# First expert tile in other PSUM banks, and a later place for GpSimd's last product of a stage

## What is computed

```python
# state-space block, per batch: 512 channels, 16 states, 512 time steps
u     = silu(conv4(in_proj @ ctx))
delta = softplus(dt_proj @ dt_low + bias)
state = state * exp(delta * A) + (delta * u) * B      # a scan over time
y     = sum over the 16 states of state * C, plus D * u
x     = x + tanh(g) * (y * silu(layernorm(x)))
# layer 0's feed-forward: 16 experts, 4 for each token, and a shared one
x     = x + tanh(g) * (sum of w_e * ((silu(x @ G_e) * (x @ U_e)) @ D_e) + shared)
# layer 1's feed-forward: a dense matmul and low-rank experts, 2 of 8
```

## Time and profile before

| | |
|---|---|
| median of 3 runs | 1559.41 us (1557.27 to 1560.66) |
| profiled execution: time, span | 1560.78 us, 1559.0 us |
| TensorE busy | 1263.5 us (81%) |
| VectorE busy | 1413.8 us (91%) |
| ScalarE busy | 835.8 us (54%) |
| GpSimd busy | 794.4 us (51%) |
| mean granted TensorE clock | 0.922 of full |
| DMA | 264.27 MB, mean 170 GB/s |

### The profile page before, as it was taken

The page is one execution under the profiler, slowest core; times in us unless marked ns, Lnnn a source line. Parts: engine busy times, 40 slices in busy tenths (PEclk is TensorE's granted clock), DMA queues, the critical chain, the costliest instruction groups (busy, mean ns, idle before and its releaser), DMA issues.

```text
span 1559.0 us, 13944 instructions
## 1 busy us (share of the span) xinstructions
PE 1263.5 (81%) x4244; PEld 701.1 (45%) x4244; DVE 1413.8 (91%) x1462; ACT 835.8 (54%) x1341; POOL 794.4 (51%) x413
## 2 busy tenths in 40 slices
PE   6785687799699868987869999889998889923888
PEld 2322232343244324442526666566665666612444
DVE  4999999999999999988896999999899999977894
ACT  5754747564765456534864765546655444423442
POOL 0465456545654553350464455655556655565642
PEclk7898899999989988998978999999999999975999
DMA  7354456535553543350465678666887877854531
GB/s 252 96 135 128 106 129 142 140 103 143 140 137 91 146 129 102 91 164 23 94 177 186 237 257 259 234 249 234 268 244 234 280 258 283 267 161 139 164 106 55
DMA packets 99835, 264.27 MB, mean 170 GB/s; under 512 B 10833, under 2 KB 11345, under 8 KB 93617
## 3 DMA queue, kind: packets, MB, share of 16 engines
q1 hardware_dynamic: 87936, 225.36, 49.4%
q0 software_dynamic: 11440, 37.50, 7.2%
q10 hardware_dynamic: 384, 0.52, 0.1%
HBM read 233.73 MB, written 29.62 MB: 169 GB/s over the span
## 4 chain that ended last, share of the span: by engine, by line
DVE 42%; PE 24%; issue 9%; DMA 6%; POOL 5%; ACT 2%; DVEq 0%; SPq 0%; ACTq 0%; POOLq 0%
DVE state L1615 18%; DVE banks L1607 12%; PE banks L1108 8%; PE banks L1119 3%; DMA expert_w<-in_moe_w 3%; PE banks L1018 3%; POOL state L448 2%; DMA ys_d<-expert_out 2%; DVE y_scan L1626 2%; PE banks L1261 2%; PE banks L1067 1%; PE banks L1075 1%; PE banks L1087 1%; DVE du L1331 1%; DVE small L1385 1%
## 5 line engine op out<-in xcount | busy, mean ns | idle before, releaser
L448 POOL TENSOR_TENSOR state<-state,bc_rows 128x1024 f32<-128x1024 f32 x256 | 606.6, 2371 | 659.3 <-DVE banks L1607 659.2
L1018 PE MATMUL banks<-state,ident 128*128 128x512 f32 x640 | 338.1, 660 | 118.2 <-POOL state L448 118.2
L1615 DVE TENSOR_TENSOR_SCAN state<-decay,banks 128x1024 f32<-128x1024 f32 x176 | 402.1, 2285 | 7.0 <-ACT decay L673 1.7
L1607 DVE TENSOR_TENSOR banks<-du,bc_rows 128x1024 f32<-128x1024 f32 x256 | 315.2, 1231 | 12.8 <-issue 0.5
L1108 PE MATMUL banks<-z_gate,expert_w 128*128 128x256 f32 (+1 forms) x1504 | 287.1, 349 | 6.4 <-DMA expert_w<-in_moe_w 5.7
L1108 PEld LDWEIGHTS banks<-z_gate,expert_w 128*128 128x128 f32 x1504 | 251.5, 192 | 61.2 <-issue 21.3
L1018 PEld LDWEIGHTS banks<-state,ident 128*128 128x128 f32 x640 | 121.3, 204 | 307.9 <-POOL state L448 194.4
L673 ACT ACTIVATE decay<-delta,neg_a 128x511 f32<-128x511 f32 x352 | 230.7, 712 | 53.9 <-DVE state L1615 45.9
L1615 DVE TENSOR_TENSOR_SCAN state<-expert_w,banks 128x1024 f32<-128x1024 f32 x80 | 182.9, 2286 | 6.8 <-ACT expert_w L673 4.2
L1119 PE MATMUL banks<-expert_w,hidden 128*128 128x512 f32 x316 | 156.9, 612 | 2.9 <-DVE hidden L1636 2.9
L1626 DVE TENSOR_TENSOR y_scan<-y_scan,state 128x1024 f32<-128x1024 f32 x96 | 118.4, 1234 | 3.3 <-POOL state L448 3.3
(11 more groups left out here) (303 smaller groups left out, 1590.5 us busy)
## 6 DMA issues: line engine op xcount, KB each, us to landing
bc_rows<-bc_d SPq DMA_DIRECT2D x208, 512.0 KB, 5.0
expert_w<-in_moe_w SPq DMA_DIRECT2D x48, 1536.0 KB, 9.0
ys_d<-expert_out SPq DMA_DIRECT2D x32, 512.0 KB, 10.2
ctx_t<-in_ctxT SPq DMA_DIRECT2D x8, 512.0 KB, 6.8
x_res<-in_x SPq DMA_DIRECT2D x4, 1024.0 KB, 10.7
xn_d<-y_scan SPq DMA_DIRECT2D x4, 1024.0 KB, 7.4
ys_d<-expert_out SPq DMA_DIRECT2D x15, 256.0 KB, 9.5
out_x<-x_res SPq DMA_DIRECT2D x3, 1024.0 KB, 5.6
```

The costliest lines, as they stand in the source:

```text
L448: nc.gpsimd.tensor_tensor(W[:, c % 4], W[:, c % 4], bcast2(BC[:, u, 1, :]), ALU.mult).then_inc(mulc_done, 1)
L1018: mm = nc.tensor.matmul(PS[:, m], ID[:, :], W[:, c % 4, m, :], start=False, stop=True, skip_group_check=True)
L1607: nc.vector.tensor_tensor(drive(s), DU[:, s % 2, 2 * h:2 * h + 2, :], bcast2(BC[:, u, 0, :]), ALU.mult).then_inc(mulb_done, 1)
L1615: nc.vector.tensor_tensor_scan(flat(W[:, c % 4]), flat(DAS[c % da_slots(s, i)]), flat(drive(s)), 0.0, ALU.mult, ALU.add).then_inc(scan_don ...
```

## The change

Three parts.

1. `mul_c`: the last product of stages 0 to 3 now also waits for the first `mul_b` of the next stage. The last one of stage 4 still waits for its scan alone.
2. Tile 0 uses banks 4 and 5 for its transposes and its gate and up products (`XT(j)`, `GU(j, it)`). Its transposes stand behind the `sum_state` of the sixth unit of stage 4's last turn, and wait for the rows, for the projections' last reader and for the table's reader. ScalarE's copies (`tile_rows(0, h)`) stand ahead of stage 5's first decay. The waits for `y4_ready` and the last scan now stand behind tile 0's gate and up matmuls, ahead of tile 1's transposes.
3. GpSimd gathers tile 0 one unit earlier (behind the fourth product of stage 4's last turn), and tile 1 one unit later (behind the last product of the stage, not ahead of it).

```diff
-        XT = PS[:, 0:2].rearrange("p a (k r) -> p a k r", k=ET // 2)
+        XT = lambda j: (PS[:, 0:2] if j else PS[:, 4:6]).rearrange("p a (k r) -> p a k r", k=ET // 2)
+        GU = lambda j, it: PS[:, it if j else 4 + it]
...
-                if (k + 1) % HS and not routed:
+                if ((k + 1) % HS or s < NB) and not routed:
                     pool.wait_ge(mulb_done, k + 2)
...
-                    if i == 3 and c == 4:
+                    if i == 3 and c == 3:
                         pool.wait_ge(xn_stored, 16 * NB)
                         pool.wait_ge(index_ready, 1)
                         gather_rows(0)
-                    if i == 3 and c == 6:
+                    if i == 3 and c == 7:
                         pool.wait_ge(shgu_done, IT * NB)
                         gather_rows(1)
...
             seed(p)
+            for h in range(2):
+                tile_rows(0, h)
...
-                    if j < NTILE - 1:
+                    if 0 <= j < NTILE - 1:
                         tile_rows(j + 1, 0)
...
                 if c == 0:
                     index_round(ROUNDS - 1)
-            pe.wait_ge(y4_ready, 1)
-            pe.wait_ge(scan_done, HS * FIRST_B + PRE_SCAN)
-            for h in range(2):
-                tile_transposes(0, h)
+                if c == 5:
+                    pe.wait_ge(dt_read, ET * (FIRST_B + 1))
+                    pe.wait_ge(index_ready, 1)
+                    for h in range(2):
+                        tile_transposes(0, h)
...
                     tile_in(j)
+                    if j == 0:
+
+                        pe.wait_ge(y4_ready, 1)
+                        pe.wait_ge(scan_done, HS * FIRST_B + PRE_SCAN)
```

More of the change, by code:

```diff
@@ L722, in tile_rows @@
                 n = P * BLOCKS[j]
-                nc.scalar.activation(XST[:, 2 * h:2 * h + 2, 0:n], XT[:, h, :, 0:n], ACT.Copy).then_inc(xst_ready, 1)
+                nc.scalar.activation(XST[:, 2 * h:2 * h + 2, 0:n], XT(j)[:, h, :, 0:n], ACT.Copy).then_inc(xst_ready, 1)
             def tile_tanh(j, it):
@@ L729, in tile_tanh @@
                 n = P * BLOCKS[j]
-                nc.scalar.activation(HT[:, j % 2, it, 0:n], PS[:, it, 0:n], ACT.Tanh, scale=0.5).then_inc(sil_ready, 1)
+                nc.scalar.activation(HT[:, j % 2, it, 0:n], GU(j, it)[:, 0:n], ACT.Tanh, scale=0.5).then_inc(sil_ready, 1)
             def tile_out(j):
@@ L1086, in tile_transposes @@
                         at = (2 * h + k) * P
-                        mm = nc.tensor.transpose(XT[:, h, k, r * P:(r + 1) * P], rows_of(j)[:, r, at:at + P], ID[:, :])
+                        mm = nc.tensor.transpose(XT(j)[:, h, k, r * P:(r + 1) * P], rows_of(j)[:, r, at:at + P], ID[:, :])
                 mm.then_inc(xt_done, 1)
@@ L1107, in tile_in @@
                             at = g * WGU + k * INNER + it * P
-                            mm = nc.tensor.matmul(PS[:, it, g * TILE:g * TILE + n], MW[:, u % 2, at:at + P],
+                            mm = nc.tensor.matmul(GU(j, it)[:, g * TILE:g * TILE + n], MW[:, u % 2, at:at + P],
                                                   XST[:, k, 0:n], start=(k == 0), stop=(k == ET - 1))
@@ L1632, in tile_hidden @@
                 dve.wait_ge(sil_ready, j * 2 + it + 1)
-                nc.vector.scalar_tensor_tensor(out=h, in0=h, scalar=1.0, in1=PS[:, it, 0:n], op0=ALU.add,
+                nc.vector.scalar_tensor_tensor(out=h, in0=h, scalar=1.0, in1=GU(j, it)[:, 0:n], op0=ALU.add,
                                                op1=ALU.mult).then_inc(hg_ready, 1)
                 dve.wait_ge(hg_ready, j * 2 + it + 1)
-                nc.vector.tensor_tensor(h, h, PS[:, it, TILE:TILE + n], ALU.mult).then_inc(h_ready, 1)
+                nc.vector.tensor_tensor(h, h, GU(j, it)[:, TILE:TILE + n], ALU.mult).then_inc(h_ready, 1)
             def shared_hidden(b, it):
```

## The result

| | before | after |
|---|---|---|
| median, same chip (6 runs each) | 1560.04 us (1556.07 to 1561.06) | 1547.88 us (1542.69 to 1549.53) |
| profiled execution: time, span | 1560.78, 1559.0 us | 1544.43, 1542.7 us |
| VectorE, TensorE busy | 1413.8, 1263.5 us | 1408.2, 1259.2 us |

The ratio is 0.992, with a 95% interval from 0.9901 to 0.994: 12.2 us faster. Forecast were 1545.5 us and a gain of 13.9.

A forecast was written before the change was run, and what follows sets the result against it. VectorE (42% of the chain) and TensorE (24%) bound the kernel by turns. A 6.4 plus B 7.5 made 13.9 us off 1559.4, so 1545.5 us; own range 1541.5 to 1549, full range 1541 to 1554.

The forecast's parts named there:

- A: Ends of stages 0 to 3: last product moved behind the next stage's first removes a collision with VectorE; 6.4 us.
- B: Start of the tiles: tile 0 in banks 4 and 5 lets hidden values start earlier; 7.5 us.
- Stages 1 and 3, 2.16 us each: Ends of stages 1 and 3: VectorE's multiply loses the collision, chain stays on VectorE; 2.16 us each, 4.3 together.
- Stage 2, 1.1 us: End of stage 2: TensorE's sum for stage 3's fifth scan is close behind, so at most 1.1 us won.
- Stage 0, 1.0 us: End of stage 0: gain between 0 and 2.6 us, given an unexplained VectorE wait of 0.46; 1.0 taken.
- The price of 2.16 us at stage 4's end: End of stage 4: the last product, behind tile 1's gather, collides with VectorE's second sum or multiply; costs 2.16 us.
- rival 1: End of stage 4: product gets in only after VectorE's four queued instructions, B 3.8 us; 1549.2 us; chance 0.13.
- The two cancel: Last turn of stage 4: tile 0's earlier gather delays the fifth product 0.6 us; 0.61 regained at the sixth.
- Tile 0, wait gone: Start of stage 5's tiles: VectorE's first hidden values start 7.3 us earlier with TensorE's clock up, 5.8 otherwise.
- Does it last: Stages after the tile start run the same course, earlier; tile 1's weights arrive in time, nothing subtracted.
- Rivals 3 and 4: Tiles: transfer waits take B back, 1553.0 us, chance 0.11; TensorE falls to low clock, 1566 us with 8 tiles, chance 0.07.
- Rival 2: Stages 1 to 3: TensorE or ScalarE comes last, leaving 2 of A's 6.4 us; 1549.9 us; chance 0.13.

The follow-up runs named there:

- the later silu: Changed kernel with ScalarE's gate silu moved from a stage's end to behind the next stage's second decay: 1543.19 us, ratio 0.9896.
- the second repeat: The changed kernel itself, unmodified, measured once more against the kernel before: 1547.94 us, ratio 0.9933.
- the repeat with the old gathers: Changed kernel with the gathers of tiles 0 and 1 back behind the fifth and seventh product, measured again: 1544.02 us, ratio 0.9914.
- the first repeat of the change: The changed kernel itself, unmodified, measured again against the kernel before: 1548.5 us, ratio 0.993.

## Why the prediction was right, and where its terms were off

The time lies in the forecast's own range, and the mechanism was the forecast one: no rival came to pass as described. That the sum came so near is in part luck. The steps add up to 13.7 us where the sum had 13.9, but A gave 1.2 more than forecast and B 1.4 less, and the two errors cancel; the 12.2 us of the medians are 1.5 less again, which is within their spread. The terms:

- **Stages 1 and 3, 2.16 us each: size right for the multiply, short of it at stage 1.** 1.28 came in the profile. The step that failed is "the chain stays on VectorE": I had looked at TensorE as the engine close behind and not at ScalarE, whose second table load ends 1.3 us before the first scan's decays do. That it is a limit is shown by the later silu at the three ends where ScalarE was as late as here (tanh waits of 4.09, 4.09 and 3.92 us): all three gave 2.16 or 2.17. Without it the steps into stages 2 and 3 ran from 0.13 to 2.18; with the scan's wait for the decay added, each makes 2.2 again.
- **Stage 2, 1.1 us: right by number, wrong by reason.** -1.22 came, but from the decay of the first scan (0.98 us of wait), not from TensorE's sum at the fifth. In four of the profiles without the silu's move the end gave 2.16 or 2.17, so the 1.1 us of slack that I took from rows 4 did not bind: the sum came earlier too. In the second repeat it is over 2.2 us ahead of the fifth scan (478.15 against 480.34), not 1.1.
- **Stage 0, 1.0 us: mis-sized.** 2.16 came, in every profile with the product held. The unseen 0.46 us is a delay that moves along with its surroundings, not a wait for a fixed time.
- **Missed: the fifth scan of stage 1**, 0.75 us. Before, it waited for TensorE's sum:

```profile
200.88 2.29 DVE L1615 TENSOR_TENSOR_SCAN state<-decay,banks 128x1024 f32<-128x1024 f32 x1 [0.79 <-PE banks L1018]
```

Every profile with A has a step of 0.67 to 0.76 there, the two without A have none. So A was 7.6 us in the profile, where the sum had 6.4.

- **The price of 2.16 us at stage 4's end: right**, as "one long VectorE instruction" (4.61 us for the two sums). This also decides rival 1, that VectorE keeps the port: the last product stands directly behind the one before it and got in between VectorE's instructions. The lengths are those of one engine standing still while the other runs: 3.38 = 1.22 + 2.16 for VectorE, and 5.62 - 2.35 = 3.27 for the product against 2.35. The rule of the Trainium skill that the prediction cites ("SBUF — State Buffer", section on the two separate sides), a lock held for the whole instruction, agrees with these lengths. That one product gets in between two VectorE instructions that stand back to back is what the rows add. The prediction had this price from the gather that part 3 puts behind the product. What it did not weigh is the kernel with the new banks and the old gathers: while the gather stood ahead of the last product, it kept the product away from the sums, and that kernel has no such step and 8.4 us at the tiles. "The two cancel", on the gather of tile 0, came true: +0.71 and -0.61 at the last two scans of stage 4.
- **Tile 0, wait gone: right.** VectorE finds the hidden values ready, as the case "clock up" had it: it takes them 16.2 us after the start of the stage's last scan, where it was 23.6, so 7.4 us earlier, forecast 7.3. TensorE's first tile matmul comes 5.3 us after the stage's last scan (804.59 less 799.27), forecast some 6.
- **B in sum, 7.5 us: 6.1 in this profile** (2.16 - 10.00 + 1.70), 6.9 and 6.8 in the repeats. Up to the third scan it is right: 7.8 us. The step that failed is the one to tile 1, which TensorE was to reach "up to 0.7 us earlier still"; VectorE waits 3.52 us for it there, not under 1.83, and 1.70 us are lost again. I had costed tile 1's weights and not its rows, which part 3 puts behind the last product: they landed 9.65 us after the second gather's end (805.91 to 815.56), and TensorE stood for 3.90 us.
- **"Does it last": nearly.** From the fifth scan of stage 5 to the last scan the steps stay within 0.8 us, and what follows is 1.1 us longer. The prediction's own sign starts earlier, at the first hidden values, with 2 us allowed: that stretch is 729.5 us where it was 727.2, so 2.4 longer, most of it the 1.70 above; in the repeats it is 0.6 and 1.5 longer. Rivals 3 and 4 did not come; the mean clock is 0.928 where it was 0.922. Rival 2 came in small: ScalarE kept 0.9 us at each of two ends.

One sentence of the prediction gives 2.43 us of TensorE's idle time with rows 2; the row shown there is that of the weight load, with 3.25, and 2.43 belongs to the matmul that follows it.

## What to carry to other kernels

When two engines get in each other's way at one point, ask for each instruction moved away from there what it had kept apart: the gather that was moved behind the product had been the spacer that kept it off VectorE's sums. Where a change removes a pause, look at all engines that feed the next instruction, the table loads of ScalarE among them, since the one that is second by 1 us becomes the limit. And read a change of a few us by its steps from one profile to the other before the medians. Where VectorE alone decides, the steps repeat here to 0.02 us (2.16 at a stage end, 10.00 at the tile); where ScalarE or TensorE comes last, they vary with the clock (0.13 to 2.18, 0.87 to 1.70). An edit is tested only at a place where the wait that it is to remove would have been there.

## What the runs showed of the hardware that I had not expected

**The clock's steps are as large as the effects looked for.** Some profiles gain 1.62 us at the 14th scan of stage 4 or 2.0 to 2.6 us at the fifth of stage 6, and others of the same kernel don't. The 14th scan in the profile of before:

```profile
689.21 2.29 DVE L1615 TENSOR_TENSOR_SCAN state<-decay,banks 128x1024 f32<-128x1024 f32 x1 [1.66 <-ACT decay L673]
```

In the 8 us ahead of it TensorE's granted clock is 0.79. The five profiles with the step have 1.00 there and no wait; the other eight have 0.79 and a wait of 1.65 to 1.71 us.

At the fifth of stage 6 four matmuls of the input projection stand in the chain. The window over them in the profile of before (us, busy PE, PEld, DVE, ACT, POOL, granted clock, DMA share, GB/s):

```profile
1032.50:1035.50 3.00, 3.00 (x5) 1.22 (x4) 2.96 (x3) 1.81 (x3) 0.50 (x1) 0.57 0.32 109
```

Their row in its timeline:

```profile
1032.52 3.17 PE L959 MATMUL banks<-ctx_t,in_w 128*128 128x512 f32 x4
```

The window of the repeat with the old gathers:

```profile
1012.40:1015.40 3.00, 3.00 (x11) 1.64 (x11) 2.48 (x2) 1.62 (x3) 2.58 (x2) 1.00 0.62 214
```

And their row there:

```profile
1013.79 1.88 PE L963 MATMUL banks<-ctx_t,in_w 128*128 128x512 f32 x4
```

In both, TensorE has waited for VectorE's hidden values (before: 2.71 and then 1.08 us; here 2.71 alone) and runs at 0.50 of the clock for the 3 us ahead of the window; then in the one it stays mostly at 1.2 GHz, in the other it is back at 2.4 GHz. From the end of the 2.71 us to the tile's next matmuls it takes 8.38 us in the one and 5.84 in the other. The step is missing in the first and third profile of the changed kernel and is there in the second; it is in 9 of the 13 profiles of changed kernels. What decides it is not settled; none of my edits switched it reliably. It is the likely reason why single executions of one program lie far apart (13.2 us for the kernel before on one chip), since the mean granted clock goes with the time: of the 46 executions of that kernel beside the experiments, the 11 with 0.923 or less have a median of 1563.5 us, the 23 with 0.927 or more 1555.4. That it is also why two edits with sure steps did not add up in the medians is argued, not shown.

**ScalarE's wait hangs on TensorE's clock.** In the kernel with the product held at stage 4 nothing was changed before stage 4, and yet ScalarE was not late at stage 2 to 3. The window from 15 to 10 us ahead of that stage's last scan (453.28) in that kernel, granted clock 1.00:

```profile
438.28:443.28 5.00, 5.00 (x13) 2.26 (x12) 4.80 (x6) 4.96 (x7) 2.36 (x1) 1.00 0.27 55
```

The same stretch in the first repeat of the change (last scan 456.05), 0.50:

```profile
441.05:446.05 5.00, 5.00 (x8) 2.27 (x8) 4.80 (x6) 4.65 (x5) 2.36 (x1) 0.50 0.22 54
```

ScalarE's tanh of the shared expert waits there for TensorE, and the silu behind it ran from 451.89 us in the first and from 458.03 in the second, 1.4 us before and 2.0 us after the start of the stage's last scan. All 14 profiles agree on it, at both ends (stage 1 to 2 and 2 to 3): where the clock of that stretch is 1.00, the tanh waits 2.39 us (14 ends); where it is 0.50 to 0.68, 3.7 to 5.4 us (14 ends). With the silu at its old place it starts 1.4 us before the last scan in the first case and 1.2 to 2.4 us after it in the second.

**A gather's issue has two lengths.** In one kernel, the changed one, the two issues of tile 1's gather occupied GpSimd for 1.79 us (at 802.86, beside VectorE's sum) and 0.95 us (at 804.96, beside its first product of stage 5), for the same bytes. What VectorE's instruction has to do with it was not tried.
